# x times W as seven block products over pairs of batches in a first phase, and everything behind h in a second

## What is computed

```python
result = jnp.einsum('bsd,od->bso', x, base_weight) + base_bias
h = jnp.einsum('bsd,brd->bsr', x, A)
result = result + jnp.einsum('bsr,bor->bso', h, Bw)
...
query = hidden_states @ Wq.T
router_scores = (query @ Wr.T) @ (aux_keys @ Wr.T).T / np.sqrt(RDIM) + log_rel
top_scores, top_idx = jax.lax.top_k(router_scores, 8)
attn = query @ aux_keys.T / np.sqrt(BOT) + log_rel   # on the 8 chosen slots
w = jax.nn.softmax(attn, axis=-1)
aux_out = (w @ aux_values) @ Wvd.T @ Wvu.T
u = clip(log_var / mean(log_var) * 0.5 + sigmoid(gelu(h @ Wu1.T + bu1) @ Wu2.T + bu2) * 2.5, 0, 5)
gate = sigmoid(gate_w1 * u_norm + gate_bias)
out = x + h + gate * aux_out
```

## Time and profile before

| | us |
|---|---|
| median of three runs | 2120.66 |
| the profiled execution | 2120.01 |
| its span in the trace | 2118.2 |
| TensorE busy | 2095.7 |
| VectorE busy | 1217.3 |
| ScalarE busy | 793.2 |
| GpSimd busy | 2.5 |

### The profile page before, as it was taken

One profiled execution on the slowest core, in us unless ns is written; L12 is line 12 of the kernel. 1 busy time (PEld: TensorE's weight loads), 2 busy tenths in 40 slices (PEclk: granted clock), 3 DMA queues, 4 the chain that ended last, 5 costly groups with the idle time before them and its releaser, 6 DMA issues.

```text
span 2118.2 us, 25447 instructions
## 1 busy us (share of the span) xinstructions
PE 2095.7 (99%) x9510; PEld 1728.6 (82%) x9510; DVE 1217.3 (57%) x1995; ACT 793.2 (37%) x1193; POOL 2.5 (0%) x10
## 2 busy tenths in 40 slices
PE   7999999999999999999999999999999999999998
PEld 5888788888888888888888888888888788888886
DVE  4544655665575556656665565557556744444445
ACT  4433533443353334333533353335334432222221
POOL 0000000000000000000000000000000000000000
PEclk9999999999999999999999999999999999999999
DMA  7444544453445444544553445345444366666668
GB/s 247 170 157 155 174 157 138 139 195 126 145 153 180 137 132 164 168 145 136 162 171 127 154 141 190 129 145 172 157 139 136 125 190 222 221 222 218 220 227 304
DMA packets 161009, 359.47 MB, mean 170 GB/s; under 512 B 21172, under 2 KB 22196, under 8 KB 160758
## 3 DMA queue, kind: packets, MB, share of 16 engines
q1 hardware_dynamic: 105590, 257.16, 38.6%
q10 hardware_dynamic: 55296, 100.69, 12.4%
HBM read 257.11 MB, written 100.66 MB: 169 GB/s over the span
## 4 chain that ended last, share of the span: by engine, by line
PE 95%; DVE 2%; DMA 1%; ACT 1%; issue 0%; SPq 0%; ACTq 0%; DVEq 0%
PE bank L1109 22%; PE bank L1111 21%; PE bank L1110 21%; PE bank L1165 6%; PE bank L1167 5%; PE bank L1166 5%; PE bank L1128 1%; PE bank L1045 1%; PE bank L1046 1%; PE bank L1035 1%; PE bank L1036 1%; PE bank L1201 1%; PE bank L1200 1%; PE bank L1199 1%; PE bank L1087 1%; PE bank L1075 1%
## 5 line engine op out<-in xcount | busy, mean ns | idle before, releaser
L1109 PE MATMUL bank<-xh,wsp 128*128 128x512 f32 x2048 | 803.2, 392 | 2.8 <-DVE wsp L688 1.6
L1111 PE MATMUL bank<-xh,wsp 128*128 128x512 f32 x2048 | 798.1, 390 | 0.0
L1110 PE MATMUL bank<-xl,wsp 128*128 128x512 f32 x2048 | 797.7, 389 | 0.0
L1109 PEld LDWEIGHTS bank<-xh,wsp 128*128 128x128 f32 x2048 | 384.9, 188 | 83.5 <-DVE wsp L688 2.5
L1111 PEld LDWEIGHTS bank<-xh,wsp 128*128 128x128 f32 x2048 | 384.7, 188 | 81.3
L1110 PEld LDWEIGHTS bank<-xl,wsp 128*128 128x128 f32 x2048 | 385.1, 188 | 78.6
L688 DVE TENSOR_TENSOR wsp<-wraw,wsp 128x1024 fp32r<-128x1024 f32 (+1 forms) x387 | 322.5, 887 | 181.8 <-ACT wsp L426 181.8
L426 ACT ACTIVATE wsp<-wraw 128x1024 fp32r<-128x1024 f32 (+1 forms) x258 | 266.9, 1079 | 358.4 <-PE bank L1046 357.1
L793 DVE TENSOR_TENSOR stage<-stage,xl 128x512 f32<-128x512 f32 x128 | 88.6, 692 | 447.6 <-ACT stage L572 447.6
L572 ACT ACTIVATE stage<-bank,bias_sb 128x512 f32<-128x512 f32 x128 | 88.1, 688 | 543.1 <-PE bank L1128 543.1
L1165 PE MATMUL bank<-h_sp,xh 128*128 128x512 f32 x512 | 201.7, 394 | 1.9 <-DVE h_sp L688 1.9
(11 more groups left out here) (137 smaller groups left out, 1676.5 us busy)
## 6 DMA issues: line engine op xcount, KB each, us to landing
wraw<-in_w SPq DMA_DIRECT2D x129, 544.0 KB, 4.8
wraw<-in_w SPq DMA_DIRECT2D x129, 512.0 KB, 3.5
xraw<-in_x SPq DMA_DIRECT2D x136, 256.0 KB, 5.1
h_dram<-stage ACTq DMA_DIRECT2D x128, 256.0 KB, 2.0
r_dram<-stage ACTq DMA_DIRECT2D x128, 256.0 KB, 2.3
xraw<-h_dram SPq DMA_DIRECT2D x128, 256.0 KB, 3.1
xraw<-r_dram SPq DMA_DIRECT2D x120, 256.0 KB, 3.9
out<-stage ACTq DMA_DIRECT2D x112, 256.0 KB, 4.0
```

The costliest lines, as they stand in the source:

```text
L1109: pe.matmul(acc_ps, w_hi, xh[:, k, :], start=(k == 0), stop=False)
L1110: pe.matmul(acc_ps, w_hi, xl[:, k, :], start=False, stop=False)
L1111: last_k = pe.matmul(acc_ps, w_lo, xh[:, k, :], start=False, stop=False)
```

## The change

The program is rewritten throughout; the inputs, the splitting into three matmuls and the arithmetic behind h are the same.

*Phase 1.* Batches are taken in pairs. For one pair, x is a 2 x 2 arrangement of half-feature blocks (two batches by two halves of the 2048 inputs) and W one of two halves by two halves. Seven products M1, M2, M6, M7, M4, M5, M3 (one level of the Strassen scheme in Winograd's form) replace the eight block products. Each has 8 output blocks ("tiles", 224 in all) with 8 values of k. The sums of W (T1 to T4) are formed in the first pair by GpSimd (`make_t1` and so on) and go to DRAM (`t_dram`) for the later pairs; those of x (S1 to S4) GpSimd forms in every pair. VectorE adds the products' results up in `u_t` and `v_t` (`combine`) and makes h with the bias (`finish`, at k = 3 of the next tile, behind `lora_b`). There are four PSUM banks for the tiles, three slots of split weights, three of raw ones (`wraw`), 12 tiles of split x. Here only h is stored; query and router are no longer part of phase 1.

*Phase 2* has 10 rows of 16 steps. In a step: `aux_pass` (one at most, 31 steps behind, in one bank up to the last batch's first block), the router's matmuls where they are due, `u_pass` (12), `query_pass` (2), and in four steps per batch `attention_pass`, which now uses the bank of the scores. Batch c - 1's router is done in row c, its outputs begin at step 15 of that row. Rows 8 and 9 have no `u_pass`. The gate is multiplied into the softmax weights (`normalise`), so it is no longer transposed. x + h is formed by GpSimd in phase 2 from x and h, both loaded again. ScalarE's exponential and its gelu and tanh now alternate, each batch with two table loads.

```diff
-                        w_hi = wsp[:, slot, k * P:(k + 1) * P]
-                        w_lo = wsp[:, slot, WCOL + BOT + k * P:WCOL + BOT + (k + 1) * P]
-                        pe.matmul(acc_ps, w_hi, xh[:, k, :], start=(k == 0), stop=False)
-                        pe.matmul(acc_ps, w_hi, xl[:, k, :], start=False, stop=False)
-                        last_k = pe.matmul(acc_ps, w_lo, xh[:, k, :], start=False, stop=False)
...
+M1, M2, M6, M7, M4, M5, M3 = range(NPROD)
+H_PRODUCTS = (M2, M4, M5, M3)
...
+        T1_AT, T2_AT, T4_AT, T3_AT, T1B_AT = -1, HT, 2 * HT, 3 * HT - 3, 5 * HT - 4
+        entries = []
+        for g in range(TILES):
+            p, q, o = tile_of(g)
+            when = g - 2
+            if p == 0 and q == M6:
+                entries.append((T4_AT + o, 1, "t4", g))
+                continue
+            if p == 0 and q == M2:
+                entries.append((T2_AT + o, 1, "t2", g))
+            if p == 0 and q == M7:
+                when = T3_AT + o
+            if p == 0 and q == M5:
+                when = T1B_AT + o
+            entries.append((when, 0, "tile", g))
...
+                if n >= NWR:
+                    _, _, old, og = entries[n - NWR]
+                    if old == "tile":
+                        p, q, o = tile_of(og)
+                        sp.wait_ge(wl_ready, og + 1)
+                        if p == 0 and q == M1:
+                            sp.wait_ge(t_ready, t_count("t1", o))
+                        if p == 0 and q in (M7, M5):
+                            wait_stored(sp, "tile", og)
+                    elif old == "t2":
+                        sp.wait_ge(t_ready, t_count("t2", og % HT))
+                    elif old == "t4":
+                        wait_stored(sp, "t4", og)
...
+            def make_t3(o):
+                g = M7 * HT + o
+                wait_w(pool, "tile", g)
+                pool.wait_ge(t_ready, t_count("t2", o))
+                pool.tensor_tensor(w_raw("tile", g), w_raw("tile", g), t_res[:, o, :], SUB).then_inc(t_ready, 1)
...
+                    make_s1(p, o)
+                if q == M5:
+                    make_s4(p, o)
+                if q == M3 and p < NPAIR - 1:
+                    make_s3(p + 1, o)
...
+                    src = w_raw("tile", g)
+                to_hi(wsp[:, g % NW, 0, :], src).then_inc(wh_ready, 1)
+                if p == 0 and q == M6:
+                    act.dma_start(t_dram[T2, o], src).then_inc(t2_out, 16)
+                if p == 0 and q == M7:
+                    act.dma_start(t_dram[T3, o], src).then_inc(t_out[W_PLACE["tile", g] % NWR], 16)
+                if p == 0 and q == M5:
+                    act.dma_start(t_dram[T1, o], src).then_inc(t_out[W_PLACE["tile", g] % NWR], 16)
+
+            def store_t4(o):
+                act.wait_ge(t_ready, t_count("t4", o))
+                act.dma_start(t_dram[T4, o], w_raw("t4", M6 * HT + o))\
+                    .then_inc(t_out[W_PLACE["t4", M6 * HT + o] % NWR], 16)
...
+                if q == M7:
+                    dve.wait_ge(main_done, g + 1)
+                    dve.wait_ge(u_ready, HT * p + o + 1)
+                    dve.wait_ge(xl_ready, x_index(p, M7, o) + 1)
+                    dve.wait_ge(s2_ready, HT * p + o + 1)
+                    dve.tensor_tensor(v_t[:, o, :], ps, u_t[:, o, :], ADD).then_inc(v_ready, 1)
...
+                if q == M5:
+                    pe.wait_ge(u4_ready, HT * p + o + 1)
+                pe.matmul(main_ps[g % NBANK][:], b_sp[:, chunk % 2, (o % 4) * P:(o % 4 + 1) * P], ax[:],
+                          start=False, stop=True, skip_group_check=True).then_inc(lb_done, 1)
...
+                for k in range(HT):
+                    i = x_index(p, q, k)
+                    if k == 0:
+                        pe.wait_ge(wl_ready, g + 1)
+                    if o == 0:
+                        pe.wait_ge(xl_ready, i + 1)
+                    f = slice(k * P, (k + 1) * P)
+                    pe.matmul(ps, wsp[:, slot, 0, f], x_hi(i), start=(k == 0), stop=False)
+                    pe.matmul(ps, wsp[:, slot, 0, f], x_lo(i), start=False, stop=False)
+                    last = pe.matmul(ps, wsp[:, slot, 1, f], x_hi(i), start=False, stop=(k == HT - 1))
...
-                wait(pe, topk, TOPK_STEPS * i)
-                tok = slice(t * P, (t + 1) * P)
-                pe.matmul(sc_ps[:], qa[:, tok], g_a[:], start=True, stop=False)
-                pe.matmul(sc_ps[:], qb[:, tok], g_b[:], start=False, stop=True)
-                pe.matmul(at_ps[:], qa[:, tok], k_a[:], start=True, stop=False)
-                pe.matmul(at_ps[:], qb[:, tok], k_b[:], start=False, stop=True).then_inc(scores_done, 1)
...
+                wait(pe, topk, TOPK_STEPS * i)
+                tok = slice(t * P, (t + 1) * P)
+                pe.matmul(s_ps[:], qa[:, tok], g_a[:], start=True, stop=False)
+                pe.matmul(s_ps[:], qb[:, tok], g_b[:], start=False, stop=True).then_inc(sc_done, 1)
+
+            def attention_pass(i):
+                t = i % TT
+                pe.wait_ge(topk, TOPK_STEPS * i + 2)
+                tok = slice(t * P, (t + 1) * P)
+                pe.matmul(s_ps[:], qa[:, tok], k_a[:], start=True, stop=False)
+                pe.matmul(s_ps[:], qb[:, tok], k_b[:], start=False, stop=True).then_inc(at_done, 1)
...
-            def gate_pass(c):
-
-                wait(pe, gate_step, GATE_STEPS * (c + 1))
-                wait(pe, zg_ready, c)
-                for t in range(TT):
-                    last = pe.transpose(gate_ps[:, t * P:(t + 1) * P],
-                                        gt[:, t:t + 1].broadcast_to([P, P]), ident[:])
-                last.then_inc(gate_done, 1)
...
+            def aux_pass(a):
+                b, o = a // KT, a % KT
+                pe.wait_ge(zl_ready, (b + 1) * (TT // 2))
+                if a == 0:
+                    pe.wait_ge(vul_ready, 2)
+                wait(pe, out_ready, a if a <= (NB - 1) * KT else max((NB - 1) * KT + 1, a - 3))
...
-            def masked(i):
-
-                wait(dve, topk, TOPK_STEPS * i + 2)
-                dve.tensor_scalar(rep[:], rep[:], SENTINEL, MASKED, ALU.not_equal, ALU.mult)\
-                    .then_inc(topk, 1)
-                wait(dve, topk, TOPK_STEPS * i + 3)
-                wait(dve, wt_done, i)
-                dve.tensor_tensor(att[:], at_ps[:], rep[:], ALU.add).then_inc(topk, 1)
-                wait(dve, topk, TOPK_STEPS * i + 4)
-                dve.tensor_reduce(nmax[:], att[:], AX.X, ALU.max, negate=True).then_inc(topk, 1)
...
+            def masked(i):
+                dve.wait_ge(topk, TOPK_STEPS * i + 3)
+                dve.wait_ge(at_done, i + 1)
+                wait(dve, wt_done, i)
+                dve.tensor_tensor(att[:], s_ps[:], rep[:], ADD).then_inc(topk, 1)
+                dve.wait_ge(topk, TOPK_STEPS * i + 4)
+                dve.tensor_reduce(nmax[:], att[:], AX.X, ALU.max, negate=True).then_inc(topk, 1)
...
+                dve.tensor_scalar(att[:], att[:], rsum[:], gt[:, b % 2, t:t + 1], MULT, MULT).then_inc(wgt_ready, 1)
...
+            def add_out(a):
+                dve.wait_ge(aux_done, a + 1)
+                dve.wait_ge(r_ready, a + 1)
+                wait(dve, out_in[a % 4], 16 * (a // 4))
+                dve.tensor_tensor(o_st[:, a % 4, :], aux_bank_of(a)[:], r_h[:, a % 4, :], ADD).then_inc(out_ready, 1)
...
+            def load_r(a):
+                b, o = a // KT, a % KT
+                if a == 0:
+                    sp.wait_ge(main_done, TILES)
+                    sp.wait_ge(wl_ready, TILES)
+                wait(sp, r_ready, a - 3)
+                sp.dma_start(r_x[:, a % 4, :], x[b, o]).then_inc(rx_in[a % 4], 16)
+                wait(sp, out_ready, a - 3)
+                sp.dma_start(r_h[:, a % 4, :], h_dram[b, o]).then_inc(rh_in[a % 4], 16)
...
+            for a in range(NAUX):
+                pool.wait_ge(rx_in[a % 4], 16 * (a // 4 + 1))
+                pool.wait_ge(rh_in[a % 4], 16 * (a // 4 + 1))
+                pool.tensor_tensor(r_h[:, a % 4, :], r_h[:, a % 4, :], r_x[:, a % 4, :], ADD).then_inc(r_ready, 1)
...
+            for step in range(ROWS * KT):
+                c, k = step // KT, step % KT
+                b = c - 1
+                a = aux_of(step)
+                if a is not None:
+                    aux_pass(a)
+                if 1 <= c <= NB:
+                    if k == 1:
+                        learned_pass(b)
+                    if k in TURN_AT:
+                        turn_pass(b * TT + TURN_AT[k])
+                    if k in Z_AT:
+                        z_pass(b, Z_AT[k])
+                    if k in SCORE_AT:
+                        score_pass(b * TT + SCORE_AT[k])
+                if c == 0 and k == 1:
+                    stats_pass(3 * NPAIR - 1)
+                if c == 0 and k == 8:
+                    pe.wait_ge(mstep, 5)
+                    pe.matmul(mean_ps, ones[:], rowsum[:], start=True, stop=True).then_inc(mean_done, 1)
```

(23 more changed lines are left out.)

1939 lines of the change are left out of this document (1088 added, 851 removed).

## The result

The changed kernel takes **2236.7 us** (median; 2234.0 to 2239.5) against 2120.7 for the kernel before, a ratio of 1.0547 (95% interval 1.0529 to 1.0565): 5.5% slower. The forecast was 2101 us with a range of 2066 to 2155, so direction, size and range were wrong. The profiled execution took 2234.4 us with a span of 2232.6; the sum had given 2099, so 133.6 us have to be found.

A forecast was written before the change was run, and what follows sets the result against it. TensorE was taken to bound the kernel, by matmul count times spacing plus stops. Last wu matmul at 2004.5, router chain 59.5, last outputs 30 and slow spacing 5 gave span 2099, forecast 2101 us, range 2066 to 2155.

The forecast's parts named there:

- Removed matmuls, pairs 1 to 3: Whole kernel: 768 fewer main matmuls, -174.1 us; in phase 1, pairs 1 to 3, VectorE keeps up, +2 us for `lora_b`.
- The rival of the lost phase 1: Phase 1, every pair: VectorE and GpSimd miss their dates, 1 us on 168 blocks, 2270 us; chance 0.03.
- Pair 0, +15 us, bounds 0 to 45: Phase 1, first pair: stops from GpSimd's T and S sums, two chains and a slow restart, +15 us in all.
- (b): Pair 0, M6 to M7: T4 and T3 through three `wraw` slots stop TensorE once, 9 us, plus 3 for the restart.
- (a): Pair 0, M1: the weight load waits on SyncE for T1, a cycle of 6.8 us against 5.44, +3 us.
- GpSimd's price: Pair 0: a 128x1024 sum on GpSimd taken at 2.2 us, between bounds of 1.0 and 3.7.
- The rival that had the two exclude each other: Pair 0, M2: VectorE's two-operand sums and GpSimd exclude each other, 32 us more, 2133 us; chance 0.13.
- The turn of the phases, +4.3 us: Between phase 1's last matmul and wu's first: `finish`, square, wu splits and h split, +4.3 us (3 to 8).
- The stops of phase 2, +78 and +2 us: Phase 2: 28 scoring stops of 2.4 us, 67, and 11 of smaller waits, +78 (60 to 95); GpSimd's sum +2.
- The spacing behind the stops: Phase 2: matmuls behind stops keep the 0.227 us spacing, with only 0.1 us put in for a scoring stop's restart.
- The end, 59.5 + 5 + 30: After the last wu matmul: router chain 59.5 us (52 to 80), slow spacing 5, last 16 outputs 30 (26 to 40).
- The rival of the clock: Phase 2 and last chain: clock falls at the stops, 28 x 2 = 56 us and 13 more, 2170 us; chance 0.10.

## Why the prediction was wrong, step by step

- **Removed matmuls, pairs 1 to 3.** Right: full rows at the full clock, M5's `lora_b` waited once, 2.9 us in pair 1, for the 2 us put in. The rival of the lost phase 1 did not come.
- **Pair 0, +15 us, bounds 0 to 45.** This term failed first: 80 us, beyond its upper bound. Some 55 us of it are idle time of TensorE and 15 the half clock behind its stops, where 3 had been put in. Phase 1 ended at 1441 us, not 1378: **+63**. Of the two chains that were followed, (b) at M7 was right in place and about in size (9 and 3 us forecast, 9.3 measured together). (a) was wrong in size: 6.8 us a round became 8.6, because T1 took 3.1 us, not 2.2, and its load 4.9, not 4. And the step stopped short of what is queued behind the waiting `load_w`: the x tiles of M2 and M5. Moving them ahead gave back all of the 15.7 us in M2 and 12 of the 29 in M5; the 17 that stay there weren't in the forecast either. What stands behind the wait was a reading of SyncE's queue, for which the changed program had all that was needed.
- **GpSimd's price.** 2.2 us was taken. The shortest rows give 2.34 and 2.35 us (199.09 and 83.68 us, VectorE idle when they started), the means 2.5 to 3.1. The rival that had the two exclude each other took the blocks to be full from 1.8 ns per element on; 3.1 us is 3.0. It had 0.13 and 32 us. The exclusion is real; but M2, the place that it named, had no excess left once the loads went ahead, and the 16 us that half of the sums gave back lie in M6, M7 and M5.
- **The turn of the phases, +4.3 us.** Right: 4.32 us.
- **The stops of phase 2, +78 and +2 us.** Right: 81.6 us of idle time, 2.25 us per stop, the releasers as named.
- **The spacing behind the stops.** This step failed second, **+52 us** in phase 2. A granted clock under 1 in phase 2 was one of its own signs of being wrong. It was a rival at 0.10, priced at 2 us a stop; the 14 stretches behind the 28 stops cost 20 us, 0.7 a stop, and six more stand behind the waits at a batch's start, which it didn't have. The argument against it was that the trace shows the slow spacing only at the start, and one stop of 1.5 us at the old end. The first part misread the trace: the slow spacing stands at 1649.91 too, behind waits of 0.79 and 1.75 us. Measured are 68 us at the half clock, of which 31 to 34 are lost, 6.5 us in first matmuls behind stops (0.38 us to the next start instead of 0.23, 43 times; some 4 of them were in the forecast as restarts), 4.6 in 50 single spacings of 0.28 to 0.38 us and 2.7 in slow stretches of two or three matmuls. Some 7 us of the 52 aren't placed.
- **The end, 59.5 + 5 + 30.** **+19 us**: the chain took 79.6, 15 more than the 64.5. Filling, which held the clock up, took it from 78.1 to 66.3: 12 us are the half clock, where 5 had been put in. Even filled the chain is 7 us longer than the 59.5, so the walk through the steps was 7 to 8 us short. The outputs took 33.7 for 30.

63 + 52 + 19 = 134 us, all of it. The rival of the clock came true and that of GpSimd in part, but half of pair 0's loss, the loads behind a waiting load, was in no rival. The half clock is in all three terms: the full clock was carried over from a kernel in which TensorE hardly ever waits to one in which it waits 42 times in phase 2 alone.

## What to carry to other kernels

When a change turns a TensorE that never waits into one that stops for 2 us again and again, price the stop by its idle time and by the matmuls at the half clock behind it (here 2.25 us and, on average over the 28, 0.7 us more; 1.4 where the clock fell). Look in the old trace for every place where the granted clock is under 1, however short, and at the waits ahead of it. Then look whether VectorE can do what TensorE waits for first: two moved calls gave back 83 us. In a queue that waits for a result, list everything queued behind the wait, not only the transfer that waits: issue what depends on nothing ahead of it (37 us). And take no elementwise work to GpSimd at its undisturbed price while VectorE works on two operands in SBUF.

## What the runs showed of the hardware

- VectorE's 128x1024 split took 1.225 us alone and 2.427 with GpSimd's 128x1024 subtractions beside it; a 128x512 one 0.69 and 2.88; with one operand in PSUM 0.69 and 0.68. GpSimd's own took 2.89 us there; its shortest in the changed kernel, started while VectorE was idle, 2.34.
- TensorE fell to the half clock behind 27 of 44 waits of over 2 us, with stretches of 2.5 to 3.4 us at 0.43 us spacing, and behind none of 21 that were filled with matmuls whose result nobody reads. Pairs of shorter waits with 0.7 us of work between them (0.8 to 1.7 and 1.46 us) were followed by it in 16 cases of 18, and once in the kernel before (0.79 and 1.75 us). In the last batch's chain such filling took the granted clock from 0.54 to 0.92, and the chain from 78.1 to 66.3 us.
